# A one-head attention pass that gathers each run of 128 edges once and copies the rows by step on ScalarE

## The reference, cut to what matters

```python
def _gat_layer(x, src, dst, W, a_src, a_dst, b, num_nodes):
    H, C = a_src.shape
    h = (x @ W).reshape(num_nodes, H, C)
    al_s = jnp.einsum('nhc,hc->nh', h, a_src)
    al_d = jnp.einsum('nhc,hc->nh', h, a_dst)
    logits = jax.nn.leaky_relu(al_s[src] + al_d[dst], 0.2)
    alpha = _segment_softmax(logits, dst, num_nodes)
    msg = h[src] * alpha[:, :, None]
    out = jax.ops.segment_sum(msg, dst, num_segments=num_nodes)
    return out.reshape(num_nodes, H * C) + b
h = jax.nn.relu(_gat_layer(x, src, dst, W1, att_src1, att_dst1, b1, num_nodes))   # four heads: L2a
h = _gat_layer(h, src, dst, W2, att_src2, att_dst2, b2, num_nodes)                # one head: L2b
```

## Time and profile before

| | us |
|---|---|
| median of 3 runs | 3112.09 |
| lowest, highest | 3111.56, 3118.44 |
| the profiled execution | 3121.85 |
| its span, first to last instruction | 3120.0 |
| GpSimd busy in the span | 2204.6 |
| TensorE (matmul) busy | 2179.9 |
| VectorE busy | 2091.6 |
| ScalarE busy | 1393.6 |

### The profile page before, as it was taken

The page is one execution under the profiler, slowest core; times in us unless marked ns, Lnnn a source line. Parts: engine busy times, 40 slices in busy tenths (PEclk is TensorE's granted clock), DMA queues, the critical chain, the costliest instruction groups (busy, mean ns, idle before and its releaser), DMA issues.

```text
span 3120.0 us, 45559 instructions
## 1 busy us (share of the span) xinstructions
PE 2179.9 (70%) x9551; PEld 1559.1 (50%) x9551; DVE 2091.6 (67%) x7394; ACT 1393.6 (45%) x3670; POOL 2204.6 (71%) x2445
## 2 busy tenths in 40 slices
PE   5766666947666666566666654455556899999998
PEld 3333344834444444344444444444444576666677
DVE  5665556558878876688877754444446587777767
ACT  3555555524434446344334443334443354554444
POOL 6777774567777776777777657777773777777656
PEclk8877778967777778787878655555555899999999
DMA  7666665144444442444444212222221466666511
GB/s 227 205 192 195 197 197 177 39 129 129 132 132 130 132 112 76 129 129 131 132 131 132 75 43 53 55 53 53 53 55 31 146 196 186 182 185 183 164 45 51
DMA packets 247934, 389.14 MB, mean 125 GB/s; under 512 B 58944, under 2 KB 161366, under 8 KB 247673
## 3 DMA queue, kind: packets, MB, share of 16 engines
q0 software_dynamic: 92032, 230.64, 27.9%
q1 hardware_dynamic: 155641, 155.59, 16.0%
HBM read 331.11 MB, written 54.91 MB: 124 GB/s over the span
## 4 chain that ended last, share of the span: by engine, by line
PE 41%; DVE 21%; DMA 13%; POOL 10%; issue 10%; ACT 3%; DVEq 2%; SPq 1%; POOLq 0%; ACTq 0%
PE PS L1832 17%; POOL work L707 9%; DVE ACC L1340 6%; DMA work<-t_z,srcK 5%; PE PS L1887 5%; PE PS L1753 5%; PE PS L1724 4%; DMA work<-in_x,srcTile 4%; DMA t_hot<-M 2%; DMA work<-t_x,srcK 2%; PE PS L1927 1%; PE PS L1810 1%; PE PS L1870 1%; DVE work L1284 1%; DVE work L1290 1%
## 5 line engine op out<-in xcount | busy, mean ns | idle before, releaser
L707 POOL DMA_INDIRECT work<-t_z,srcK x1248 | 1203.7, 964 | 406.1 <-issue 272.9
L1832 PE MATMUL PS<-work,M 128*128 128x260 f32 (+3 forms) x3328 | 1035.9, 450 | 235.1 <-DVE ACC L1340 161.4
L1832 PEld LDWEIGHTS PS<-work,M 128*128 128x128 f32 x3328 | 696.4, 250 | 456.7 <-issue 342.8
L1340 DVE TENSOR_TENSOR ACC<-ACC,PS 128x260 f32 (+3 forms) x1614 | 598.9, 371 | 107.2 <-PE PS L1832 23.9
L2061 ACT ACTIVATE M<-iota,dloc 128x128 f32<-128x128 f32 x1248 | 396.6, 389 | 234.5 <-PE PS L1832 234.5
L707 POOL DMA_INDIRECT work<-t_x,srcK x416 | 396.4, 953 | 127.0 <-issue 94.2
L707 POOL DMA_INDIRECT work<-in_x,srcTile x392 | 376.6, 961 | 135.0 <-issue 80.2
L1724 PE MATMUL PS<-work,M 128*128 x832 | 320.6, 531 | 157.8 <-ACT work L2024 77.5
L1724 PEld LDWEIGHTS PS<-work,M 128*128 128x128 f32 x832 | 184.3, 253 | 286.5 <-issue 267.3
L1311 DVE TENSOR_TENSOR work<-work 128x256 f32<-128x256 f32 x800 | 306.7, 424 | 27.5 <-ACT work L2051 26.4
L1753 PE MATMUL PS<-Y,w 128*128 x832 | 266.3, 404 | 28.3 <-DVE wz L1216 20.0
(11 more groups left out here) (267 smaller groups left out, 2892.4 us busy)
## 6 DMA issues: line engine op xcount, KB each, us to landing
work<-t_dhot SPq DMA_DIRECT2D x416, 128.0 KB
t_hot<-M SPq DMA_DIRECT2D x104, 256.0 KB, 4.2
M<-t_hot SPq DMA_DIRECT2D x104, 256.0 KB, 2.9
work<-t_z,srcK POOLq DMA_INDIRECT x1248
t_dhot<-work SPq DMA_DIRECT2D x104, 128.0 KB
work<-t_edge SPq DMA_DIRECT2D x104, 64.0 KB, 3.9
work<-t_x,srcK POOLq DMA_INDIRECT x416, 3.1
t_z<-Y SPq DMA_DIRECT2D x50, 130.0 KB, 1.9
```

The costliest lines, as they stand in the source:

```text
L707: pool.indirect_dma_start(out=slots[:, j, 0:width], out_offset=None, in_=table[:, :], in_offset=bass.IndirectOffsetOnAxis(ap=sources[:, k: ...
L1340: ins = vec.tensor_tensor(sums, sums, PS[k % SUMS[stage]][:, 0:cols], ALU.add)
L1832: mm(PS[k % n][:, 0:cols], M[:, k % (4 * G), :], slots_of[:, k % RING[stage], 0:cols], start=True, stop=True)\
```

## The change

The pass L2b gathers by run, as L0 does: 392 gathers with `srcTile` instead of 416 with `srcK`. The rows land in 44 slots `runs`, which lie in the unused second half of the ring's slots. Gather k from the 45th on waits until step k - 19 has been copied (`row_copied`). SyncE, behind each load of destination one-hots, waits for four gathers and then adds 4 to the semaphore `runs_in`. ScalarE copies, for each of the 416 steps, the 65 words of the step's run into the step's slot of the ring; for that it loads the run's slot into a register (16 at a time, from `slotI`) and the number of runs that the step needs (one at a time, from the new table `needI`), and waits until `runs_in` has reached that register. VectorE's logits wait for the copies of the group instead of the gathers. The setup makes one table more. The diff:

```diff
--- before.py
+++ after.py
@@ -158,6 +158,8 @@
         ROWW = D + 2
         rows = lay(0, [44, D + 1]).rearrange("p (j c) -> p j c", c=D + 1)
         ring = lay(0, [48, GATW]).rearrange("p (j c) -> p j c", c=GATW)
+        RUNS = {"L0": 44, "L2b": 44}
+        runs = ring[:, 0:RUNS["L2b"], GATW // 2:GATW // 2 + HID + 1]
         xring = lay(0, [48, ROWW]).rearrange("p (j c) -> p j c", c=ROWW)
         LG = Yf[:, 0:STEPS * 4].rearrange("p (k h) -> p k h", h=4)
         srcK = sb("srcK", [P, STEPS], I32)
@@ -228,15 +230,15 @@
         alike = lay(12496, [P], parts=ROWS)
         dst_each = lay(12624, [ROWS])
         t_edge8 = nc.dram_tensor("t_edge8", [SPARTS, ROW], U8, kind="Internal").ap()
-        TILE_TABLES = 3
+        TILE_TABLES = 4
         srcTile = sb("srcTile", [P, PADDED], I32)
         late = (2 * G + 1) * STEPS
         wTile = Yf[:, late:late + PADDED]
         LAP = RING["L0"] // G
         lap = sb("lap", [EP, 1])
-        slotI = Yf[0:1, late + PADDED + STEPS:late + PADDED + 2 * STEPS].bitcast(I32)
-        tauI = Yf[0:1, late + PADDED + 2 * STEPS:late + PADDED + 3 * STEPS].bitcast(I32)
-        assert late + PADDED + 3 * STEPS <= at[0]
+        assert late + PADDED <= at[0]
+        slotI = sb("slotI", [1, STEPS], I32)
+        needI = sb("needI", [1, STEPS], I32)
         nextI = sb("nextI", [EP, 1], I32)
         onePeps = sb("onePeps", [P, 1])
 
@@ -418,6 +420,8 @@
         pool_scaled = signal("pool_scaled", each_of(["L1", "L2a"], HELPED // 4))
         step_summed = signal("step_summed", each_of(SUMMING, STEPS))
         sum_added = signal("sum_added", each_of(SUMMING, STEPS))
+        row_copied = signal("row_copied", {"L2b": STEPS})
+        runs_in = signal("runs_in", {"L2b": PADDED})
         spread_landed = [signal(f"spread_landed{i}", {"L0": 16 * NG}) for i in range(4)]
         dst_apart = signal("dst_apart", {"L0": CHUNKS})
         dsthot_made = signal("dsthot_made", {"L0": CHUNKS, "L3": CHUNKS})
@@ -500,14 +504,14 @@
 
         PASSES = [(x, D, None, "L0"), (t_z1, D + HEADS, "L0", "L1"), (t_z2, D + HEADS, "L1", "L2a"),
                   (t_z3, HID + 1, "L2a", "L2b"), (t_x, D, "L2b", "L3")]
-        LOT = {"L0": 4, "L1": GS, "L2a": GS, "L2b": GS, "L3": 4}
-
-        GATHERS = {**each_of(SUMMING, STEPS), "L0": PADDED}
+        LOT = {"L0": 4, "L1": GS, "L2a": GS, "L2b": 4, "L3": 4}
+
+        GATHERS = {**each_of(SUMMING, STEPS), "L0": PADDED, "L2b": PADDED}
 
         def landing(stage, k):
 
-            lots = RING[stage] // LOT[stage]
-            return (group_landed if stage in GAT else row_landed)[k // LOT[stage] % lots]
+            lots = RUNS.get(stage, RING[stage]) // LOT[stage]
+            return (group_landed if stage in ("L1", "L2a") else row_landed)[k // LOT[stage] % lots]
 
         landed_before, landed_so_far = {}, {}
         for stage in SUMMING:
@@ -519,7 +523,7 @@
         def landed(eng, stage, k):
 
             mark, lot = landing(stage, k), LOT[stage]
-            eng.wait_ge(mark.sem, landed_before[stage].get(mark, 0) + 16 * lot * (k // RING[stage] + 1))
+            eng.wait_ge(mark.sem, landed_before[stage].get(mark, 0) + 16 * lot * (k // RUNS.get(stage, RING[stage]) + 1))
 
 
         def helper(stage, k):
@@ -690,18 +694,20 @@
                     if writer == "L0":
 
                         pool.wait_ge(kept.sem, kept.at(writer, BLOCKS))
-                slots = {"L0": rows, "L3": xring}.get(stage, ring)
+                slots = {"L0": rows, "L2b": runs, "L3": xring}.get(stage, ring)
                 if stage == "L3":
                     nc.gpsimd.memset(xring[:, :, D:D + 1], 0.0).then_inc(ends_set.sem, 1)
                     nc.gpsimd.memset(xring[:, :, D + 1:D + 2], 1.0).then_inc(ends_set.sem, 1)
                     pool.wait_ge(ends_set.sem, 2)
-                many = RING[stage]
-                sources = srcTile if stage == "L0" else srcK
+                many = RUNS.get(stage, RING[stage])
+                sources = srcTile if stage in RUNS else srcK
                 for k in range(GATHERS[stage]):
                     j = k % many
                     if k >= many and stage == "L0":
 
                         pool.wait_ge(step_summed.sem, step_summed.at(stage, k - many + BLOCKS))
+                    elif k >= many and stage == "L2b":
+                        pool.wait_ge(row_copied.sem, row_copied.at(stage, k - many + BLOCKS))
                     elif k >= many:
                         pool.wait_ge(step_summed.sem, step_summed.at(stage, k - many + 1))
                     pool.indirect_dma_start(
@@ -806,6 +812,10 @@
                             sp.wait_ge(picked.sem, picked.at(stage, G * (c - 3)))
                         sp.dma_start(dsthot[:, c % 4, :], t_dhot[:, c * ROW:(c + 1) * ROW])\
                             .then_inc(dsthot_moved[c % 4].sem, 16)
+                    lot = c - 4
+                    if stage == "L2b" and 0 <= lot < PADDED // LOT["L2b"]:
+                        landed(sp, "L2b", LOT["L2b"] * lot)
+                        sp.sem_inc(runs_in.sem, LOT["L2b"])
                     d = c - 7
                     if d < 0 or stage in GAT:
                         continue
@@ -913,7 +923,8 @@
             assert done[0] == SOURCES_AT
             dve.wait_ge(tiles_turned.sem, tiles_turned.at("setup", 2))
             vec.tensor_copy(wTile, PS[6][:, 0:PADDED]).then_inc(tile_tables.sem, 1)
-            vec.tensor_scalar(slotI, PS[7][0:1, 0:STEPS], 1.0, None, ALU.subtract).then_inc(tile_tables.sem, 1)
+            vec.tensor_scalar(slotI[:], PS[7][0:1, 0:STEPS], 1.0, None, ALU.subtract).then_inc(tile_tables.sem, 1)
+            vec.tensor_copy(needI[:], PS[0][0:1, 0:STEPS]).then_inc(tile_tables.sem, 1)
             step(vec.scalar_tensor_tensor(dloc[:], stepB, -float(P), PS[2][:, 0:STEPS], ALU.mult, ALU.add))
             settled()
             step(vec.tensor_copy(wK[:], PS[3][:, 0:STEPS]))
@@ -1190,7 +1201,10 @@
                         dve.wait_ge(picked.sem, picked.at(stage, GS * (g + 1)))
                         ins = vec.tensor_reduce(by_step(A), pick.rearrange("p i (c h) -> p i h c", c=PARTS), AX, ALU.add)
                     elif q == 2:
-                        landed(dve, stage, GS * g)
+                        if stage == "L2b":
+                            dve.wait_ge(row_copied.sem, row_copied.at(stage, GS * (g + 1)))
+                        else:
+                            landed(dve, stage, GS * g)
                         previous(1)
                         ins = vec.tensor_tensor(by_step(L), by_step(A), ring[:, slot:slot + GS, width:width + heads], ALU.add)
                     elif q == 3 and early:
@@ -2067,14 +2081,42 @@
             def gat_edges(stage):
 
                 heads, width = HEADS_OF[stage], WIDTH[stage]
+                places = [None]
+
+                def row_of_step(table, k, least, most):
+
+                    _, values = nc.values_load_multi_w_load_instructions(
+                        table[0:1, k:k + GS], engines=(act.engine,), min_val=least, max_val=most,
+                        skip_runtime_bounds_check_because="the table was made from the steps' numbers")
+                    return values
+
+                def copy_rows(first, last):
+
+                    for k in range(first, min(last, STEPS)):
+                        if k % GS == 0:
+                            places[0] = row_of_step(slotI, k, 0, RUNS[stage] - 1)
+                        act.wait_ge(runs_in.sem, act.value_load(needI[0:1, k:k + 1], min_val=1, max_val=PADDED))
+                        if k >= RING[stage]:
+                            act.wait_ge(step_summed.sem, step_summed.at(stage, k - RING[stage] + 1))
+                        sc.activation(ring[:, k % RING[stage], 0:HID + 1], at_block(runs, places[0][k % GS]), ACT.Copy)\
+                            .then_inc(row_copied.sem, 1)
+
+                if stage == "L2b":
+                    copy_rows(0, GS)
                 for g in range(NG):
+                    if stage == "L2b":
+                        copy_rows(GS * (g + 1), GS * (g + 1) + 4)
                     spread_hots(stage, 4 * g)
                     spread_hots(stage, 4 * g + 1)
                     spread_hots(stage, 4 * g + 2)
+                    if stage == "L2b":
+                        copy_rows(GS * (g + 1) + 4, GS * (g + 1) + 8)
                     if g:
                         fade_open(stage, g)
                     put_alphas(stage, g)
                     spread_hots(stage, 4 * g + 3)
+                    if stage == "L2b":
+                        copy_rows(GS * (g + 1) + 8, GS * (g + 2))
                     for k in range(GS * g, GS * (g + 1)):
                         if helper(stage, k) != "scalar":
                             continue
```

## The result

The changed kernel takes **3139.26 us** (median of 4 runs, 3138.61 to 3141.34), the kernel before beside it 3113.18 us (4 runs, 3111.56 to 3118.44): ratio 1.008, 95% interval 1.0068 to 1.0092. It is slower by 26 us where a gain of 27 us was forecast. The profiled execution took 3138.61 us, its span 3136.7 (before 3121.85 and 3120.0).

A forecast was written before the change was run, and what follows sets the result against it. GpSimd's gathers at 1.2544 us each were taken to bound L2b. 3121.85 - 30.1 + 1.9 + 0.6 = 3094.2 us profiled, or 3084.5 from the median; forecast 3085.5 us, range 3078 to 3180 us.

The forecast's parts named there:

- The gathers: GpSimd in L2b: 24 gathers fewer at 1.2544 us each, so the last starts 30.1 us earlier.
- the window of 44 holds GpSimd: Rival, L2b's first 5 groups: gathers wait for late copies, up to 2 us a group; 3095 us, chance 0.05.
- The price of a copy: ScalarE's sequencer: c = 0.37 us a copy, 0.25 without the register load plus 0.12 for it.
- the spread at L1711: 26 loads in L0 spread from 1.11 to 1.71 us under DMA traffic; taken as a sign of 16 small trips.
- The cover: ScalarE: three one-hot chunks, 5.6 us, cover most of four copies, so only 12 of 16 copies count.
- my formula: ScalarE's group takes 10.0 + 12c us; gathers stay the limit up to c = 0.74.
- My other sum: ScalarE's group fully serial: 9.9 + 1.1 + 16c us, within 18.9 us up to c = 0.49.
- An average for a limit: Gathers' pace in L2b: 391 x 1.2544 / 26 = 18.9 us taken for each group.
- landed long before: SyncE's waits for lots ahead of the next one-hot load: each lot is four chunks older, already landed.
- The path's end: Behind L2b's last gather: SyncE's count and ScalarE's last four copies add about 1.9 us, up to 6 if costlier.
- Rival 1: Register load's trip costs, not the word: 1.10 us, ScalarE bounds; 3272 us. Chance 0.21 for loads of 0.6 to 1.1.
- a load in between: Rival: register load of 0.5 to 0.6 us, groups between 18.9 and 20.07 us; around 3105 us, chance 0.09.

The follow-up runs named there:

- the repeats: The kernel before and the changed kernel, each run once more unchanged: ratios 1.0002 and 1.0085 to the kernel before.
- Loading twice: Changed kernel with each step's need loaded and checked twice, the first value unused: ratio 1.0745, 3350 us.
- spreading the copies: Changed kernel with copies in smaller lots, so four places a group, not two, have a copy right behind a one-hot chunk (seams): ratio 0.9988.
- The constant wait: Changed kernel without loads of needs; ScalarE waits for the constant k + 1 runs at step k: ratio 0.9988.
- quad with moved loads: Changed kernel with one need loaded for four copies, SyncE only counting and ScalarE issuing the destination one-hot loads: ratio 0.9931, 3094.7 us.
- cheap loads: Changed kernel with one need loaded for four copies, one-hot loads still on SyncE: ratio 0.9954.
- the early count: SyncE counts each lot one chunk earlier, ahead of its wait for picks: ratio 1.0041 on the changed kernel, 0.9963 with one need for four copies.
- the two fastest kernels: Changed kernel with ScalarE issuing one-hot loads, and one need loaded for four copies (3094.7 us) or 16 needs in one load (3093.85 us).

## Why the prediction was wrong

**The gathers: right.** 392 at 1.2531 us, never held (the 104 waits for copies are 0.3 us each, the usual gap). Counted from the first, the last one came 30.6 us earlier than before (29.8 between the repeats), for 30.1 forecast. The rival that the window of 44 holds GpSimd didn't come true. Nor did 1.10 us a load.

**The price of a copy: the first term that failed.** I took c = 0.25 + 0.12 = 0.37 us; it is 0.716. The load is 0.276 us, not 0.12, the register operation and the check behind it 0.170, not 0.12, and the waits, the issue and what lies between the rows some 0.2 us, where I had put 0.08. The address's 0.055 was right. I treated the load as all words (0.07) or all trip (1.10) and moved towards one end on the spread at L1711. It is both: from 1 word in 0.276 and 16 in 1.029 us, 0.05 us a word and 0.23 for the trip. Two points fix a line and can't test it, but neither end was right. The Trainium skill, Runtime: NRT & Kernel Launch, Instruction fetch mechanics, gives about 200 ns a register even in bulk; the trace has 276 ns for one register, which is near it, and 64 ns a register for 16, which is not. My estimate from that figure, 0.45 us a copy, would have left my sum as it was, too.

**The cover: the second step that failed, and at the measured c the one that decided the sign.** At the measured c my formula still says 10.0 + 12 x 0.716 = 18.6 us, quicker than the 18.9 of the gathers, and I had the limit at 0.74. The group measured 20.36. From the timeline above: 2.0 for the fourth chunk, 9.7 for 12 copies (with 1.03 us of slots and a wait of 0.6 for a count), 5.6 for three chunks, 2.3 for four copies, 1.0 for the alphas, in sum 20.6 (this one group; 20.36 is usual). The four copies that I had hidden behind one-hots cost 2.3 us. Loading twice (16 x 0.535 us a group) and spreading the copies (0.74 us for two more seams) both show it. Neither error alone turns the sign: with c = 0.37 and all 16 copies counted my sum gives 10.0 + 16 x 0.37 = 15.9 us. My other sum, the fully serial one, gives 11.0 + 16 x 0.716 = 22.5 us and had its limit at c = 0.49; the measured group lies between the two, and I relied on the lower one.

**An average for a limit: the third.** I took 391 x 1.2544 / 26 = 18.9 us as the gathers' pace in each group. While run equals step, a group wants 16 gathers, 20.07 us; later ones want fewer. The constant wait shows it from one side (20.0 to the last), quad with moved loads from the other (20, then 16.4 to 20.6). So ScalarE had to be quicker in late groups than 18.9, to catch up what the first ones can't give. An engine at 20.36 throughout keeps nothing of the 30 us: 26 x 20.36 = 529 us, more than the 523.3 of before.

**SyncE: "landed long before" was wrong twice.** Its counts stand behind waits for picks, which makes the loop of the first seven groups, 10.1 us, which I hadn't seen, though the order of the code shows it. And with cheap loads its waits for lots delay the one-hots: TensorE's picks wait 36.1 us for them, 77.4 with the early count.

**The path's end.** I had the last logits 1.9 us later behind the last gather's end than the 1.75 of before, 3.65 in sum. In the changed kernel it is 51, nearly all of it the backlog of ScalarE; in the two fastest kernels, without a backlog, 5.6 and 4.4 us. So the term was too small by one or two us, as the prediction allowed.

**The 26 us.** The two repeats on a chip each have spans of 3116.5 and 3143.8 us, 27.3 apart: L2b starts 1.9 us later, takes 19.6 us more (611.65 for 592.04; 19.3 of these up to the last logits, 10.1 of them the loop and the rest the 20.36), from there to the last store it is 2.5 us more, and the end 3.3. The 1.9 and 2.5 lie in parts that the change doesn't touch, but for the one table more in the setup (0.57 us, as forecast), and are within what executions differ by; the 3.3 is open. Rival 1 had it right that ScalarE would become the bound, by a load of 0.6 to 1.1 us, which didn't come true. The rival "a load in between" had the mechanism (ScalarE just above the gathers) at too long a load (0.5 to 0.6 us) with the sign still a gain; since it and the forecast shared the formula, both were too short by the same 1.8 us a group. The gain itself was where the forecast had it: with 26 wide loads in place of 416 narrow ones, and the one-hots moved, L2b is 28 us shorter, for 28.2 forecast there (30.1 - 1.9), and the kernel 22.8.

## What to carry to other kernels

Work that a value in memory decides costs its sequencer time, not the engine's: here 0.7 us for a copy of 0.26. Load such values many at a time, check them once, and count the sequencer's time by whole groups, with nothing hidden behind an instruction that still waits for a semaphore. Where a change speeds up the bound engine, look at the pace group by group, not on average, and follow each count back through the queue of the engine that makes it.

## What the runs showed of the hardware

- A register load on ScalarE took 0.276 us for one word and 1.029 for 16; the check of a value's bounds added 0.147 to 0.152 us of register operations and 0.018 of an assertion, more than half of the load again.
- A register load started only when the last instruction ahead of it with a wait of its own had been released, and ran ahead of those without: ScalarE's 5 to 7 ns behind the start of L2079 (50 of 50 in L2b, changed kernel), VectorE's 0.03 us behind that of L1300 and ahead of nine scalings (26 of 26 in L2b, before).
- Indirect gathers took the same time from start to start whether they fetched 65 words a row or 256: 392 in L2b from 1832.8 to 2322.8 us are 1.253 each, 416 in L3 from 2444.3 to 2965.1 are 1.255 (changed kernel).
- Programs with 416 more copies on ScalarE, and their register instructions, ended 6.9 us behind the start of their last store instead of 3.7. The cause is open.
